# A gated attention and expert block on one core: who issues two stores, the places of the last ranks and slots, and tile 2 in two passes

## The reference, cut to what matters

```
x = x + tanh(g_xattn) * attention(layernorm(x), ctx)          # this is h
x = x + tanh(g_ffn)  * mean over the token's top 2 experts of
                       relu(layernorm(h) @ W_e[expert] + b_e[expert])
```

## Time and profile before

| what | us |
|---|---|
| median of 3 runs | 342.99 |
| the profiled execution | 344.42 |
| its span, first to last instruction | 342.5 |
| PE busy | 319.5 (93%) |
| DVE busy | 203.9 (60%) |
| ACT busy | 122.9 (36%) |
| POOL busy | 75.3 (22%) |

### The profile page before, as it was taken

How to read it: one execution, slowest core, us unless ns; L and a number is a source line. 1 busy time by engine, 2 the same in 40 slices (tenths; PEclk the granted TensorE clock), 3 DMA queues, 4 the chain that set the end, 5 groups by cost and what they waited for, 6 DMA issues and landing times.

```text
span 342.5 us, 4328 instructions
## 1 busy us (share of the span) xinstructions
PE 319.5 (93%) x1510; PEld 235.1 (69%) x1510; DVE 203.9 (60%) x434; ACT 122.9 (36%) x165; POOL 75.3 (22%) x91
## 2 busy tenths in 40 slices
PE   5699999999999999959999999999999999999970
PEld 5344565565665588738788888888888888888850
DVE  2324457676668886886694975755176575753220
ACT  2223434625534558013345535515032551431000
POOL 6000110100103320303334321530120333011120
PEclk9969999999999999999999999999999999999995
DMA  7999999999948799567999999998359989634152
GB/s 253 303 288 303 349 353 332 354 319 362 389 156 292 268 382 327 147 225 206 379 340 367 353 355 354 255 381 273 61 169 346 282 215 382 208 61 63 10 84 31
DMA packets 24711, 90.57 MB, mean 264 GB/s; under 512 B 3276, under 2 KB 3276, under 8 KB 24680
## 3 DMA queue, kind: packets, MB, share of 16 engines
q1 hardware_dynamic: 13752, 52.86, 43.6%
q0 software_dynamic: 7792, 25.47, 28.5%
q10 hardware_dynamic: 3136, 11.83, 10.4%
HBM read 73.63 MB, written 16.52 MB: 263 GB/s over the span
## 4 chain that ended last, share of the span: by engine, by line
PE 80%; DMA 10%; DVE 4%; POOL 1%; ACT 1%; issue 1%; SPq 0%; DVEq 0%
PE ps L449 49%; PE ps L357 11%; PE ps L382 11%; DMA hn_rows<-hn 4%; PE ps L432 4%; DMA wg<-in_L_ffn_W_gate 3%; DMA xg<-hn_rows,src_token 2%; PE ps L403 2%; PE ps L394 1%; PE ps L348 1%; DVE stats L738 1%; DVE x_all L789 1%; DMA x_all<-in_x 1%; PE ps L365 1%; POOL guess L1117 1%
## 5 line engine op out<-in xcount | busy, mean ns | idle before, releaser
L449 PE MATMUL ps<-wh,xh 128*128 128x512 f32 x256 | 83.0, 400 | 0.1
L449 PE MATMUL ps<-wl,xh 128*128 128x512 f32 x256 | 80.4, 393 | 0.3 <-issue 0.3
L881 DVE TENSOR_TENSOR wl<-raw,wh 128x1024 fp32r<-128x1024 f32 x64 | 75.6, 1219 | 8.4 <-ACT wh L632 8.1
L449 PE MATMUL ps<-wh,xl 128*128 128x512 f32 x256 | 80.2, 393 | 0.0
L632 ACT ACTIVATE wh<-raw 128x1024 fp32r<-128x1024 f32 x64 | 63.7, 1051 | 22.9 <-DMA raw<-in_L_ffn_W_e 20.9
L449 PEld LDWEIGHTS ps<-wl,xh 128*128 128x128 f32 x256 | 48.0, 188 | 11.4 <-DVE wl L881 0.7
L449 PEld LDWEIGHTS ps<-wh,xl 128*128 128x128 f32 x256 | 48.0, 188 | 10.7
L449 PEld LDWEIGHTS ps<-wh,xh 128*128 128x128 f32 x256 | 46.4, 188 | 9.3 <-DVE xl L885 0.5
L1065 POOL DMA_INDIRECT out_rows<-y,dst_token x15 | 29.0, 1933 | 107.1 <-DVE y L895 88.5
L635 ACT ACTIVATE xh<-ps 128x1024 fp32r<-128x1024 f32 x16 | 16.4, 1024 | 90.1 <-PE ps L432 90.1
L357 PE MATMUL ps<-kT,qT 128*100 128x361 f32 x128 | 43.4, 493 | 1.0 <-ACT qT L611 1.0
(11 more groups left out here) (124 smaller groups left out, 240.0 us busy)
## 6 DMA issues: line engine op xcount, KB each, us to landing
raw<-in_L_ffn_W_e SPq DMA_DIRECT2D x64, 512.0 KB, 9.2
kT<-in_ctx_cols SPq DMA_DIRECT2D x16, 722.0 KB, 11.3
ctx<-in_ctx ACTq DMA_DIRECT2D x8, 1024.0 KB, 11.1
bias<-in_L_ffn_b_e SPq DMA_DIRECT2D x8, 512.0 KB, 10.9
ctx<-in_ctx ACTq DMA_DIRECT2D x8, 420.0 KB, 14.5
hn_rows<-hn POOLq DMA_DIRECT2D x8, 400.0 KB, 9.5
out_rows<-x_all POOLq DMA_DIRECT2D x2, 1600.0 KB, 19.1
x_all<-in_x SPq DMA_DIRECT2D x7, 384.0 KB
```

Source lines behind the costliest of these rows:

```text
L449: mm = nc.tensor.matmul(into[:, n * HB:(n + 1) * HB], rows[:, k, :], weights[:, k, n * HB:(n + 1) * HB], start=(k == 0 and c == first), st ...
L881: nc.vector.tensor_tensor(wl[e % 2][:, k, :], raw[e % 2][:, k, :], wh[e % 2][:, k, :], ALU.subtract).then_inc(s_wl, 1)
```

## The change

- The two stores of h on POOL's queue become one DMA of all eight batches on ACT's queue, issued behind the last `hn`.
- The two DMAs of zeros go from POOL's queue to SP's, behind the weights of expert 1.
- In tile 0's LH pass, `ranks(7)` moves from behind chunk 4 to behind chunk 0, `slots(6)` from chunk 2 to chunk 1, and `slots(7)` with `counts(1)` from tile 1's chunk 1 to tile 0's chunk 6.
- DVE splits the first chunk of expert 1's low weights between `locate(7)` and `name_tokens(1)`.
- Tile 2 takes HH and HL of all chunks first, waiting for `xh` alone, and LH of all chunks then. `s_wfree` is given in the first pass; a new semaphore, `s_wh0free`, tells in the second that `wh0` is free, and ACT waits for it before it writes expert 2's `wh`. The turn of tile 3 moves to chunk 5 of the first pass.
- POOL waits for h's store ahead of the first further tile's gather instead of behind it.

```diff
+            sp.wait_ge(s_const, 1)
+            for t in range(HALVES):
+                rows = out[N_TOK + t * P:N_TOK + (t + 1) * P, :].rearrange("p (a d) -> p a d", d=256)
+                sp.dma_start(rows, zero[:, :].unsqueeze(1).to_broadcast([P, D // 256, 256])).then_inc(s_zero, 16)
 
             sp.wait_ge(s_hn, B)
-            sp.wait_ge(s_hstore, 16 * len(STORES))
+            sp.wait_ge(s_hstore, 16)
             load_bias(0)
...
                 mm = tile(0, k, (LH,), LH)
-                if k == 2:
+                if k == 0:
+                    ranks(B - 1)
+                if k == 1:
                     slots(B - 2)
-                if k == 4:
-                    ranks(B - 1)
+                if k == 6:
+                    slots(B - 1)
+                    counts(1)
...
+                if n == 2:
+
+                    pe.wait_ge(s_xh, n + 1)
+                    for k in range(KD):
+
+                        tile(n, k, (HH, HL), None).then_inc(s_wfree, 1)
+                        if k == 5:
+                            turn_tile(n + 1)
                 pe.wait_ge(s_xl, n + 1)
...
-                    mm = tile(n, k)
+                    mm = tile(n, k, (LH,)) if n == 2 else tile(n, k)
                     if half == 1:
-                        mm.then_inc(s_wfree, 1)
+                        mm.then_inc(s_wh0free if n == 2 else s_wfree, 1)
                     if n + 1 < N_TILES:
-                        if k == 2:
+                        if k == 2 and n > 2:
                             turn_tile(n + 1)
...
+                if e == 2:
+                    act.wait_ge(s_wh0free, k + 1)
...
             normalise_hidden(B - 1)
+
+            act.wait_ge(s_h, B)
+            act.dma_start(out[0:N_TOK, :].rearrange("(b q) d -> q b d", q=Q), x_all[:, :, :]).then_inc(s_hstore, 16)
             split_tile(1)
...
             locate(B - 1)
+
+            split_weights(1, 0)
             name_tokens(1)
-            for k in range(KD):
+            for k in range(1, KD):
                 split_weights(1, k)
...
                 store_normed(s - 1)
-                if s == B:
-                    store_hidden(*STORES[1])
-                if s + 1 == B:
-
-                    store_hidden(*STORES[0])
-                    for t in range(HALVES):
-                        rows = out[N_TOK + t * P:N_TOK + (t + 1) * P, :].rearrange("p (a d) -> p a d", d=256)
-                        g.dma_start(rows, zero[:, :].unsqueeze(1).to_broadcast([P, D // 256, 256])).then_inc(s_zero, 16)
...
             over, over_before = overs(pool, 0)
+
+            pool.wait_ge(s_hstore, 16)
             gather_first_over(0, over, over_before)
-
             pool.wait_ge(s_zero, 32)
-            pool.wait_ge(s_hstore, 16 * len(STORES))
             add_tile(0)
```

More of the change, by code:

```diff
@@ L233, in gated_block @@
         s_wfree = sem("w_used")
+        s_wh0free = sem("first_w_high_used")
         s_gath = [sem(f"gathered{t}") for t in range(2)]
@@ L262, in overs @@
                     eng.value_load(tile_table[0:1, 1, e:e + 1], min_val=0, max_val=OVER * E))
-        STORES = ((0, HALF_B), (HALF_B, B))
         FIRST_CHUNKS = {3: (0,), 4: (1,), 5: (2,), 6: (3,), 7: (4, 5), 8: (6, 7)}
@@ L541, in _ @@
                 tile(1, k, (HH, LH), None)
-                if k == 1:
-                    slots(B - 1)
-                    counts(1)
             for k in range(KD):
@@ L647, in wait_multiplied @@
                 else:
-                    eng.wait_ge(s_wfree, KD * (e + 1))
+                    eng.wait_ge(s_wh0free if e == 0 else s_wfree, KD if e == 0 else KD * (e + 1))
             def split_over(over_before, j):
@@ L902, in evacuate @@
                 else:
-                    dve.wait_ge(s_wfree, KD * (e + 1))
+                    dve.wait_ge(s_wh0free if e == 0 else s_wfree, KD if e == 0 else KD * (e + 1))
                 dve.wait_ge(s_bias[e % 2], 16 * (e // 2 + 1))
@@ L959, in _ @@
             split_tile(2)
-            dve.wait_ge(s_hstore, 16 * len(STORES))
+            dve.wait_ge(s_hstore, 16)
             dve.wait_ge(s_hn, B)
@@ L1043, in _ @@
             pool.nop().then_inc(s_const, 1)
[L1045 to L1048, removed]
             def store_normed(b):
```

## The result

The changed kernel took 348.39 us (median of 4 runs, 347.56 to 349.92) against 343.56 for the kernel before in the same comparison: ratio 1.0162, interval 1.012 to 1.0204. The forecast was 342.9 with a range of 339.6 to 347.0. The profiled execution has a span of 346.1 us for 342.5.

What follows compares the result with a forecast made beforehand. PE was taken to bound the kernel, busy 319.5 of 342.5 us. Winning 3.17 us at tile 2 and losing 3.1 at tile 4 gave span 342.4, or 342.9 against the median, range 339.6 to 347.0.

Steps and rivals of the forecast that it cites:

- The tokens: In tile 0's LH pass, earlier ranks, slots and low chunk make tokens ready at 138.1 us and not 140.0.
- the issue on ScalarE's queue: ACT's issue of h's DMA delays tile 1's `xh` and last `hnT` about 0.5 us, costed at nothing.
- The `hn` store: Last `hn` store to scratch, free of POOL's queue: 9.5 us for 15.23, landing 136.0, up to 11 us hidden.
- The gather of tile 2: Issued at 138.4, takes 7.3 us, lands at 145.7, ahead of PE at 146.24: idle time gone, -3.17 us.
- The balance of the sum: Gain at tile 2's turn given back as idle time at tile 4's: -3.17 + 3.1, span 342.4; chance 0.37.
- h's landing: h's 3.28 MB start at about 126.3 and, at 252 GB/s, land at 149.1 for 148.1; biases follow.
- Rival 2: Ten engines carry h: 24.6 us, landing at 150.9, tile 4's gather at 171.0, +1.7 us, 344.7; chance 0.18.
- Gather 4: Behind h and biases, takes 10.1 us, lands at 169.2; PE wants it at 166.1 for tile 4's turn: 3.1 us idle.
- Rival 4: The `hn` store or tile 2's gather shares engines with h, as slow as before: 343 to 344.5; chance 0.08.
- Rival 3: h at 122 GB/s or less lands 155 to 156, tile 3 waits for `xl`: +6 to +7 us, 349.5; chance 0.13.

## Why the prediction was wrong

- **The tokens: right.** 138.1 forecast, 138.0 found; the first low chunk, the slots and `name_tokens` fell where they were put. PE was ready for tile 2 at 146.23 (146.24 forecast), so the issue on ScalarE's queue cost nothing, as forecast.
- **The `hn` store: nearly right.** 9.5 forecast, 11.6 found, landing at 138.0 or just behind: "anything to 11 us is hidden" was used up, and the gather was released by the store, 0.4 us later than forecast. The reason given for the 15.2 us before, what its queue held, was only part of it: free of that the store took 11.6 us, and with h left out 4.7, so h beside it counts too.
- **The gather of tile 2: the step that failed.** "I take 7.3, since h's remainder was under way beside it before too. ... Stall gone: -3.17 us." It took 12.4. The remainder of before ran at a share of 0.34 and ended 6 us behind the gather's issue; after the change the gather was 3.25 us sooner and h ended 13 us behind its issue. The same words, "h beside it", covered two different amounts of h. I had 11.1 us as the worst case from a gather among the weights; runs in which h was beside it for all or most of its time show 9.9 to 14.3. The term is not -3.17 but +1.89. The balance of the sum (-3.17 + 3.1) was gone with it, whatever came behind.
- **The clock: not in the sum.** An idle time of 5.06 us brought the granted clock to 0.59 and 0.56 and cost 1.08 us behind it. I had seen 3.17 us pass, with the eight turns behind it in 1.09 us, and did not ask what 5 would do.
- **h's landing: right in kind, mis-sized.** 149.1 forecast from the mean rate, 152.0 found. h started 1.4 us sooner than assumed (124.88 for 126.3) and took 27.1 us for 22.8, so the size is off by 4.3 and not by 2.9. Rival 2, ten engines, had 24.6 us and a landing at 150.9: nearer, and still 2.5 us short. The Trainium skill's rule (DMA: Bandwidth & Descriptors, "Why a DMA increments its semaphore by 16 and not by 1") is that of rival 2. The trace agrees with the ten, by the share of 0.62 to 0.64.
- **Gather 4: the mechanism was there, mis-sized.** 3.1 us of idle time forecast, 0.98 found, since PE came to it late already. The gather took 12.1 us for the 10.1 assumed and landed at 173.2 for 169.2. With the idle time at tile 2 gone it is 1.10 (h as 96 and 4 rows).
- **The rivals.** Rival 4 named the right place, and put it at no worse than before. A hint was there in the earlier trace rows: the gather landed at 149.4, just behind h at 148.1, so its 7.33 us might have belonged to h. Rival 3's 349.5 lies nearest to the 348.39 measured, but by luck: its tile 3 waiting for `xl` did not come (PE stands idle only at the turns of tiles 2 and 4), and its path had no loss at tile 2.

## What to carry to other kernels

Spread a large store over all DMA engines by its rows (here 96 and 4, not 100), and read the share of the DMA windows for it: a flat 0.62 was the mark of ten of sixteen here. It pays if the store is then through before the urgent transfer starts: on GpSimd's queue, and for h issued late, it did not pay here. When a transfer is issued earlier, ask what it will then run beside, and for how long; its duration belongs to its neighbours and cannot be carried over from the place that it left. Where an engine will arrive earlier, list the next transfers that were just in time and move each ahead of waits that are not its own.

## What the runs showed of the hardware that I had not expected

- A gather of 128 rows took 4.6 us with no h beside it, 5.5 to 8.2 us beside the last 3.5 to 6.1 us of one, and 9.9 to 14.3 us beside a store of h that ran for 9 us or more of it, on ten engines or on all (14.3 at a share of 0.87 to 1.02).
- All seven idle times of 4.53 to 6.95 us before tile 2's turn ended in a turn at the lower clock (1.97 us, not 1.09; in the changed kernel the granted clock was 0.59 and 0.56 in the two stretches around it). One of 2.68 us did too, in the kernel before with 96 and 4 rows (0.85 and 0.72), while one of 3.17 us in the kernel before did not (1.00). What decides it, these runs do not tell.
- Single executions are compared better from a common point behind the start than by their spans, which carry 3.2 us of scatter from before tile 0's turn.
